# A two-layer graph kernel: four operations of each dense step in another place, and edge groups without a wait for scatters

## The reference

```
# layer 0: max over edges
e      = x[src] * (1 + softplus(coeff) * edge_weight)
pooled = relu(layer_norm(e @ pool_w + pool_b, ln_pool_g, ln_pool_b))
agg    = max(segment_max(pooled, dst), 0)
h      = relu(layer_norm(concat(x, agg) @ final_w + final_b, ln_final_g, ln_final_b))
x1     = norm(x + h)
# layer 1: relations by 8 bases, mean over edges
agg[b] = segment_sum(x1[src] * comp[edge_type, b], dst) / max(deg, 1)
out    = norm(x1 + concat(agg, x1) @ weight + bias)
```

## Time and profile before

| | |
|---|---|
| median of 3 runs | 882.5 us (880.93 to 883.58) |
| the profiled execution | 882.3 us, span 880.5 us |
| TensorE, VectorE, ScalarE, GpSimd busy | 90%, 88%, 68%, 80% of the span |
| dense stage | to about 490 us |
| edge stage | about 490 to 628 us |
| last stage | about 628 to 880 us |

### The profile page before, as it was taken

One profiled execution on the slowest core, in us unless ns is written; L12 is line 12 of the kernel. 1 busy time (PEld: TensorE's weight loads), 2 busy tenths in 40 slices (PEclk: granted clock), 3 DMA queues, 4 the chain that ended last, 5 costly groups with the idle time before them and its releaser, 6 DMA issues.

```text
span 880.5 us, 17875 instructions
## 1 busy us (share of the span) xinstructions
PE 793.3 (90%) x4519; PEld 553.4 (63%) x4519; DVE 775.1 (88%) x2703; ACT 601.5 (68%) x2887; POOL 703.4 (80%) x703
## 2 busy tenths in 40 slices
PE   4699999999999999999999999997499998989760
PEld 3577777777777777777777787775345544434340
DVE  6999999999999999999999999986179999999780
ACT  4699999999999999999999988885202121111130
POOL 2599899899899899899898577776677777777777
PEclk9899999999999999999999999999589999999895
DMA  4366676666666666676666534444187887878711
GB/s 115 107 221 221 214 241 219 214 219 221 210 219 222 209 221 218 207 222 221 211 219 199 172 123 124 134 149 144 48 291 280 321 285 287 303 271 303 270 47 46
DMA packets 90699, 179.84 MB, mean 204 GB/s; under 512 B 17161, under 2 KB 36018, under 8 KB 84326
## 3 DMA queue, kind: packets, MB, share of 16 engines
q1 hardware_dynamic: 73414, 147.26, 50.1%
q0 software_dynamic: 15744, 30.96, 11.2%
q10 hardware_dynamic: 1440, 0.50, 0.3%
HBM read 109.02 MB, written 70.91 MB: 204 GB/s over the span
## 4 chain that ended last, share of the span: by engine, by line
PE 56%; POOL 23%; issue 9%; DVE 6%; ACT 3%; DMA 3%; ACTq 0%; POOLq 0%; DVEq 0%
PE ps L586 13%; PE ps L554 13%; POOL out_rows L431 11%; POOL rows L438 11%; PE ps L565 6%; PE ps L539 5%; PE ps L611 4%; PE ps L578 4%; PE ps L548 4%; PE ps L600 3%; PE ps L610 2%; POOL x_table L486 2%; PE ps L589 2%; DMA x_table<-agg_all,scat_x 1%; ACT junk L767 1%
## 5 line engine op out<-in xcount | busy, mean ns | idle before, releaser
L767 ACT ACTIVATE junk<-ps 128x128 bf16<-128x128 f32 x884 | 233.0, 287 | 21.1 <-PE ps L589 12.3
L767 ACT ACTIVATION_READ_ACCUMULATOR junk<-ps 128x1 f32 x884 | 193.6, 219 | 0.0
L719 PE MATMUL ps<-agg_all,w_cen 128*128 128x512 f32 (+1 forms) x400 | 178.0, 599 | 3.1 <-DVE agg_all L1271 2.5
L431 POOL DMA_INDIRECT x_dst<-in_x,dst_i x98 | 153.5, 1566 | 14.9 <-issue 4.5
L586 PE MATMUL ps<-w_cen,xT 128*128 128x128 f32 x984 | 157.8, 292 | 1.4 <-ACT xT L827 1.4
L461 POOL TENSOR_TENSOR work<-work,vec_raw 128x512 f32<-128x512 f32 x98 | 124.6, 1272 | 35.4 <-DVE work L1171 24.7
L586 PEld LDWEIGHTS ps<-w_cen,xT 128*128 128x128 f32 x984 | 127.9, 195 | 30.2 <-issue 27.9
L554 PE MATMUL ps<-w_cen,work 128*128 128x128 f32 x984 | 146.2, 293 | 0.0
L1271 DVE TENSOR_TENSOR agg_all<-coefs,ps 128x1024 f32<-128x1024 f32 x98 | 117.7, 1210 | 29.7 <-PE ps L705 18.3
L554 PEld LDWEIGHTS ps<-w_cen,work 128*128 128x128 f32 x984 | 122.3, 196 | 28.8 <-issue 28.8
L1107 DVE BATCH_NORM_STATS2 bn<-work 128x6 f32<-128x128 f32 x492 | 133.0, 276 | 0.7
(11 more groups left out here) (147 smaller groups left out, 1399.8 us busy)
## 6 DMA issues: line engine op xcount, KB each, us to landing
coefs<-coef_line SPq DMA_DIRECT2D x49, 1024.0 KB, 7.4
rows<-in_x SPq DMA_DIRECT2D x97, 256.0 KB
x_table<-work SPq DMA_DIRECT2D x97, 256.0 KB, 2.1
out_rows<-outb SPq DMA_DIRECT2D x97, 256.0 KB, 2.1
x_dst_table<-x_dst SPq DMA_DIRECT2D x98, 64.0 KB
rows<-x_dst_table SPq DMA_DIRECT2D x24, 256.0 KB
apart<-apart_line SPq DMA_DIRECT2D x14, 224.0 KB
x_dst<-in_x,dst_i POOLq DMA_INDIRECT x98, 4.0
```

Of the source, the lines that this page charges most:

```text
L431: return pool.indirect_dma_start(*args, bounds_check=last_node, oob_is_err=False)
L719: last = pe.matmul(MT[b][:, 0:n * D], w_cen[:, W_BASE + m, :], prod[:, b, m, 0:n, :].rearrange("p t d -> p (t d)"), start=(m == 0), stop=( ...
L767: last = nc.scalar.activation(junk[:, kind * CH + m, :], bank[:, cols(m, m + 1)], ACT.Square, accum_out=power[:, b, 1, TOP + kind * CH + m ...
```

## The change

Four orders change for steps up to 103, or for all steps in the case of VectorE's spread, and a wait goes:

- TensorE: `first_bias` stands ahead of `rooted`, so both bias products follow each other.
- ScalarE: x1 (`first_layer`) stands ahead of the squares of the root product (`rooted`).
- VectorE: the pooled scaling stands right behind the four scalings.
- VectorE: the spread stands ahead of the residual (all steps).
- TensorE: `first_bias` no longer waits for `x1_scattered` in edge groups. The last stage's own wait for all scatters stays.

```diff
                     if is_group(c, 1):
-                        d = c - 1 - DENSE - LEAD
-                        if d >= 0:
-                            pe.wait_ge(x1_scattered[d % LEAD], 16 * CH * (d // LEAD + 1))
                         need(pe, S["dve_t"], s - 2)
...
                 if c < EDGE_ORDER:
                     turned()
                     root_bias()
+                    first_bias()
                     rooted()
-                    first_bias()
                     first_layer()
...
                     turned()
                     roots()
+                    first_layer()
                     rooted()
-                    first_layer()
                     squares()
...
-                residual()
                 if stats:
                     own.need(first)
                     spread_at = spread(RES, TOP)
+                residual()
...
                     scaled()
+                    pooled_scaled()
                     first_layer()
                     stats_of(2)
-                    pooled_scaled()
                     stats_of(3)
```

## The result

The changed kernel took 955.2 us (3 runs, 953.82 to 955.61) where 882.5 us stood before: a ratio of 1.082, 95% interval 1.079 to 1.085. It is slower by 8%. The forecast was 873 us, the range 862 to 884, and slower had a chance of 0.16.

A forecast was written before the change was run, and what follows sets the result against it. The prediction took a VectorE - GpSimd - VectorE ring to set the 4.73 us dense step. Brake -3.9, x1 -1.0, spread -3.6 and start -1.0 sum to -9.5 from 882.3: 873 us, range 862 to 884.

The forecast's parts named there:

- Pooled scaling behind the scalings: VectorE, dense step: L1164 about 0.4 us earlier, ending TensorE's wait at L600; worth nothing by itself, x1 of tile 3 0.25 later.
- held longer: slower: Rival, chance 0.15: GpSimd's L431 goes first and keeps residual L1119 waiting beyond 0.61 us; whole 1.01 us gives 915 us.
- It gets nowhere until L1119 is through: Dense step: GpSimd's gather L431 takes 1.59 us instead of 1.01 because it waits for VectorE's residual L1119.
- the sum for the spread: Dense step: residual 0.05 us behind L431, L431 1.65 us, GpSimd's ring 4.69 us; 0.04 us gained over 90 steps, -3.6 us.
- neither stops the other: Rival, chance 0.08: L431 takes 1.01 us, TensorE's 4.51 us bounds the dense step, -20 us, 856 us in all.
- TensorE alone would need 4.51 us: Dense step: TensorE's own floor, 4.73 less the 0.22 us lost waiting for `pooled` at L600.
- x1 ahead of the squares: ScalarE: worth nothing in the steady dense step; between 0 and 1.03 us at the edge stage's start, taken as -1.0.
- Brake: Edge stage: TensorE's L578 no longer waits for a scatter, closing GpSimd's holes of 3.3 and 0.57 us; -3.9 us.
- The whole is wrong if the dense step is above 4.8: Sign that the whole prediction fails: dense step below 4.6 or above 4.8 us, or scatters still taking 131 us.
- Variance at 0.17: Sign of being right: VectorE's variance L1095 in the dense step takes 0.17 and not 0.47 us.
- no wait of L578 for a scatter: Sign of being right: in the edge stage TensorE's L578 no longer stands waiting for a scatter, 3.70 us before.
- L600 right behind L565: Sign of being right: TensorE's transpose of `pooled` starts 0.55 us after the row transposes L565 in the dense step.

## Why the prediction was wrong

**The step that failed.** "Pooled scaling behind the scalings": "By itself it is worth nothing, because TensorE isn't the one that sets 4.73", and "x1 of tile 3 (L1202) comes 0.25 later, with GpSimd's and SyncE's users further behind". I asked who waits for L1202 and not what L1202 itself meets 0.25 us later. The same scalings that it follows also release L461, so its place relative to L461 was 0.16 us of lead, less than the 0.25 that I moved it. The edit alone costs 0.92 us a step, 5.65 for 4.73. I had weighed this very kind of exclusion, but only for the pair that the prediction looked at, the residual and L431.

**Order of arrival.** My "held longer: slower" rival named the right mechanism at the wrong place. The x1 tile takes 0.26 to 0.29 us when it starts at least 0.07 us ahead of the addition, and 1.25 to 1.32 us, until the addition's end, when it starts 0.03 to 0.1 us behind. The Trainium skill (SBUF — State Buffer, section Who interferes with whom) says that issue order decides who blocks, that the first holds the shared pair of ports for its whole length, and it names `tensor_scalar`, which the x1 tile is, among the operations that can take the pair. The trace agrees here, and for the residual and L452 (0.68 and 0.87 us in one order, 0.91 and 0.41 in the other).

**The reading of L431.** "It gets nowhere until L1119 is through" was the reading on which the sum for the spread rests, and it is wrong: with the residual at the same offset and the spread ahead, L431 takes 1.02. What stretched it is the residual with the small spread L1090 right behind it, and the change takes the spread out of there. So the sum's 1.65 us became 1.02, and 4.69 became 4.60: the -3.6 us for the spread were 12.1 at the first scatter (482.9 for 495.0, on different chips). The residual came 0.12 us behind the gather, where 0.05 was forecast, though the stretch from L1084 to L1119 was shorter than taken (0.27 us and not 0.36). The case "neither stops the other", given 0.08, is what happened between the residual and the gather; a residual shut out for the gather's whole length, from which the 915 us came, is not seen in any kernel. So without the failed step the forecast would still have missed: the ratio 0.977 of the kernel with the pooled scaling put back gives, as an estimate, 862 us on the chip where the kernel before takes 882.5, and not 873. The same page of the Trainium skill (SBUF — State Buffer, section Who interferes with whom) holds that a `tensor_tensor` with two SBUF inputs takes only the read side of the pair and that writing a gather's descriptors needs the write side (inferred, it says). The trace agrees for the residual alone, also an operation with two SBUF inputs (0.68 to 0.74 us, gather 1.02); it doesn't for the residual with the spread behind it (gather 1.59).

**TensorE's floor.** "TensorE alone would need 4.51 us" stands beside 4.55 us at full TensorE (before + spread, x1 ahead). The pair lowers it by up to 0.30 us, where I had put at most a tenth of each bias product. Alone it changed nothing, as predicted (4.72 for 4.73).

**x1 ahead of the squares.** "Zero" in the dense step holds from before (4.73) and fails once the spread is moved: there it is worth some 0.05 us a step, 6 us at the first scatter (482.9 to 477.0, on different chips). At the start of the edge stage I took -1.0; the wait ahead of the first scatter went from 4.43 to 4.06 in the changed kernel and to 3.96 with x1 moved alone, so 0.4 to 0.5, and with x1 moved alone the first scatter starts at 495.1 us all the same.

**Brake.** -3.9 by the sum, 2.6 us measured from first to last scatter. Both holes closed to the usual 0.30, which is the 3.9. Waits for VectorE's x1 tile at smaller holes ahead of them grew by 1.3 us together and took part of it back; about half of that is there in before + spread, bias pair too, which has the brake. The sum is inside its bounds of 2 and 7, but which part of it is the brake's was not shown by a run that changes it alone.

**The tests.** "The whole is wrong if the dense step is above 4.8": it was 5.57. "Variance at 0.17" and "no wait of L578 for a scatter" came true and said nothing of the time. L431 was 1.02 us and not 1.6, and the sign given for the slower case, a residual of over 1.3 us, did not show (0.91): the loss sat in another operation. "L600 right behind L565" did not come true in most steps. TensorE and VectorE's pooled scaling in one of them:

```profile
300.63 0.71 PE L565 MATMUL ps<-ident,rows 128*128 128x128 f32 x5
301.68 0.30 PE L597 MATMUL ps<-ident,pooled 128*128 128x128 f32 x1 [0.34 <-issue]
```

The pooled tile was done at 301.24 + 0.34 = 301.58 us (lines in the section on the result), and L597 starts 0.10 behind it, as in 54 of the 73 steps between 62 and 470 us and in all 86 of the kernel before. So the gap is the wait that the prediction took it for, but the earlier place in VectorE's order did not take it away: TensorE still comes to L597 before VectorE has made the tile.

## What to carry to other kernels

When an instruction moves by some tenths of a microsecond, look at what the other engine starts in that gap, for every pair of operations that stand beside each other, and not only at who waits for its result: if both are released by the same event, a lead of 0.16 us can be worth 1 us a step. Keep the operation that must win next to the event that releases it, and put the others behind it: here the pooled scaling, one place further down, cost nothing, and the change was then faster by 2.2%.

## What the runs showed of the hardware

- An x1 tile (SBUF to SBUF, 128x128, one tensor and per-row numbers) takes 0.26 to 0.29 us when it starts at least 0.07 us ahead of GpSimd's addition, and 1.25 to 1.32 when it starts 0.03 to 0.1 behind. The addition is hardly touched either way: 1.27 us, 1.32 at a lead of 0.08.
- VectorE's residual (both inputs in SBUF, 512 columns) and GpSimd's gather run side by side at 0.68 to 0.74 and 1.02 us, whether the residual starts 0.02 us ahead or 0.2 behind, while the same residual with a spread of 4 columns right behind it, started 0.48 to 0.64 us into the gather, makes it 0.44 to 0.62 us longer. The same spread started 0.55 us in with no residual ahead of it costs the gather nothing (1.02).
- The residual and a GpSimd operation that reads and writes SBUF (L452, 128x128): 0.68 and 0.87 us when the residual is 0.06 us ahead, 0.91 and 0.41 when it is 0.06 behind.
- One bfloat16 bias product right behind the other starts 0.22 us after it, a float32 product 0.31 us after a bias product; and the eight products ahead of a float32 product are over in 0.99 us where it was 1.09 ahead of a bias product.
